# A fused transformer stack on one core: the last sub-layer moved into a third interleaved chain

## The reference

```python
x = x + L0_xattn(ln(x), ctx, ctx, ...)   # 16 heads, each sees every 16th context token
x = x + L0_attn(ln(x), ...)              # causal, scores from distances of 3-d positions
x = x + L0_ffn(ln(x), ...)               # shared expert + 2 of 8 experts per token
x = x + L1_xattn(ln(x), ctx, ...)        # causal + cross attention + feed-forward, 3 norms
x = x + L1_attn(ln(x), ...)              # differential attention, feed-forward
x = x + L1_ffn(ln(x), ...)               # product keys: top 16 of 64 + 64, then of sums
```

```python
sim = jnp.einsum('pbnhd,hkpd->pbnhk', q, keys)       # 2 x 8 heads x 64 keys per token
sx, ix = top_k(sim[0], 16); sy, iy = top_k(sim[1], 16)
scores, pk = top_k(sx[..., :, None] + sy[..., None, :], 16)
h = gelu(x . W_down[pk]) * softmax(scores)
out = sum over heads and picks of h * W_up[pk]
```

## Time and profile before

| | us |
|---|---|
| median of 3 runs | 3579.26 (3578.63 to 3580.27) |
| profiled execution | 3580.67 |
| its span | 3578.7 |
| PE busy | 2692.9 (75%) |
| DVE busy | 1926.9 (54%) |
| ACT busy | 938.1 (26%) |
| POOL busy | 667.2 (19%) |

### The profile page before, as it was taken

How to read it: one execution, slowest core, us unless ns; L and a number is a source line. 1 busy time by engine, 2 the same in 40 slices (tenths; PEclk the granted TensorE clock), 3 DMA queues, 4 the chain that set the end, 5 groups by cost and what they waited for, 6 DMA issues and landing times. The chain is left out here.

```text
span 3578.7 us, 45769 instructions
## 1 busy us (share of the span) xinstructions
PE 2692.9 (75%) x15616; PEld 1884.7 (53%) x15616; DVE 1926.9 (54%) x7470; ACT 938.1 (26%) x2008; POOL 667.2 (19%) x572
## 2 busy tenths in 40 slices
PE   6795898478984889758986689847898489875543
PEld 3583566345762558535674457624586246752421
DVE  2313464844647437554557456484474644664457
ACT  0122242123421233222421234212332123212210
POOL 0102123012211113021140112211231211402040
PEclk9697999788996999969998799978999699985766
DMA  6174054131622226131451406323152223503100
GB/s 223 49 269 157 24 174 148 60 146 46 195 103 104 83 91 210 45 137 48 144 178 38 146 24 209 112 98 110 61 199 84 105 81 115 206 26 111 24 0 6
DMA packets 211632, 392.52 MB, mean 110 GB/s; under 512 B 83344, under 2 KB 163472, under 8 KB 186160
## 3 DMA queue, kind: packets, MB, share of 16 engines
q1 hardware_dynamic: 205232, 372.49, 30.2%
q0 software_dynamic: 6144, 16.79, 1.4%
HBM read 350.55 MB, written 38.67 MB: 109 GB/s over the span
## 5 line engine op out<-in xcount | busy, mean ns | idle before, releaser
L792 PE MATMUL ps<-xbT,stream 128*128 128x128 f32 x2560 | 343.0, 291 | 10.1 <-DMA stream<-in_experts 5.6
L792 PEld LDWEIGHTS ps<-xbT,stream 128*128 128x128 f32 x2560 | 328.1, 205 | 33.8 <-DMA stream<-in_experts 13.7
L299 POOL TENSOR_TENSOR hTB<-pb,sbuf 128x2048 f32<-128x2048 f32 x32 | 151.9, 4759 | 426.5 <-DVE pb L1650 426.5
L607 PE MATMUL ps<-cmat,aTB 128*128 128x512 f32 x256 | 158.3, 776 | 60.8 <-DVE sbuf L1734 57.1
L599 PE MATMUL ps<-ident,xnB 128*128 128x128 f32 x256 | 57.5, 337 | 169.4 <-DVE xnB L1281 125.3
L470 POOL TENSOR_TENSOR rstdA<-veA,mhalf 128x4 f32<-128x4 f32 x24 | 24.4, 1018 | 859.3 <-DVE veA L1274 859.3
L1009 PE MATMUL ps<-ident,work 128*50 128x128 f32 x32 | 12.4, 388 | 220.3 <-DVE work L1789 220.3
L510 POOL DMA_INDIRECT hTA<-y_slots,slot x64 | 62.8, 981 | 601.8 <-DMA y_slots<-yb 584.8
L805 PE MATMUL ps<-stream,hTA 128*128 128x256 f32 x640 | 163.8, 402 | 0.6 <-ACT yb L1139 0.6
L792 PE MATMUL ps<-xbT,ctxA 128*128 128x128 f32 x1280 | 157.8, 277 | 1.4 <-DMA ctxA<-in_experts 1.2
L792 PEld LDWEIGHTS ps<-xbT,ctxA 128*128 128x128 f32 x1280 | 151.4, 192 | 11.4 <-DMA ctxA<-in_experts 5.6
(11 more groups left out here) (277 smaller groups left out, 6132.3 us busy)
## 6 DMA issues: line engine op xcount, KB each, us to landing
stream<-in_experts SPq DMA_DIRECT2D x88, 1024.0 KB, 5.2
stream<-in_experts SPq DMA_DIRECT2D x88, 512.0 KB, 6.0
ctxA<-in_experts SPq DMA_DIRECT2D x40, 1024.0 KB
work<-in_ctxT SPq DMA_DIRECT2D x32, 1028.0 KB, 6.8
hTB<-in_ctxN SPq DMA_DIRECT2D x32, 1024.0 KB, 7.8
down<-in_experts SPq DMA_DIRECT2D x40, 512.0 KB
ctxA<-in_ctxT SPq DMA_DIRECT2D x16, 1024.0 KB, 9.5
stream<-in_ctxT SPq DMA_DIRECT2D x16, 1024.0 KB, 9.1
```

Of the source, the lines that this page charges most:

```text
L299: return e.tensor_tensor(out.rearrange("p (a d h) -> p a d h", a=8, d=16), a.unsqueeze(2).broadcast_to([P, 8, 16, 16]), vals[:, t, :].rear ...
L607: ins = mm(out, aT[:, k, t * P:(t + 1) * P], wt[:, k, cols], start=k == 0, stop=k == KT - 1)
L792: ins = mm(ps[:, 2 * (b % 2) + u, f * P:(f + 1) * P], wu[:, u, k, f * P:(f + 1) * P], xbT[:, b % 2, k, :], start=k == 0, stop=k == KT - 1)
```

## The change

The selection leaves `back()` and becomes a third generator, `peer()`, letter `p`, with 38 steps. `xC` is a new buffer for its residual stream. A pass `g` now runs the front of group g, the back of g-1 and the selection of g-2; at the end of a group with a back VectorE copies `xB` to `xC`. The groups are `f`, `fb` (group 1, outside the loop), six passes of `fbp`, `bp` and `p`: ten in place of nine.

The new `ORDER` begins with three steps of the selection; then each step of the front is followed by two to four of the selection, until the front is in its second norm. There the selection ends and the back starts. So the front's first norm, query and whole cross attention lie between the selection's steps. The second norm and second attention of the front lie between the steps of the back's causal and cross attention; its third norm, router and shared expert lie beside the back's first feed-forward and the norms after it, and its expert blocks beside the back's projections, differential attention and last feed-forward. After the front's last expert block come `f1h6` to `f2h4` of the back, the steps of its last feed-forward, with the front's gather and accumulation between.

`rep64`, `s16`, `cand`, `cm`, `cm2`, `phd` and `u50` now lie in the second half of `hTB`, and `rep1`, `rep2`, `cexp` and `g50` in the second half of `work`. The first halves of `ctxB` and `ctxN` and `ctxL` are loaded at the head of the pass, the second halves once the selection's last `u50` has been turned. Three waits guard the shared buffers where the back follows the selection; some waits of the selection on the back of the same group go away, since a barrier now lies between.

```diff
+        xB, xnB, xC = tiles("xB"), tiles("xnB"), tiles("xC")
...
                 for s in order(streams):
-                    next(front if s == "f" else back)
+                    next({"f": front, "b": back, "p": peer}[s])
...
+                    def first_context():
+                        contextB(0)
                         rows_of(0)
...
+                    def back():
+                        if "p" in streams:
+                            sp.wait_ge(pe_done, PE["uT", T - 1])
+                        else:
+                            first_context()
+                        contextB(1)
+                        rows_of(1)
...
+                    def peer():
+                        if "b" in streams:
+                            first_context()
...
                                 pe.wait_ge(act_done, A["cpT", t])
                                 if t >= 1:
                                     pe.wait_ge(vec_done, V["y1p", t - 1])
+                                elif "p" in streams:
+                                    pe.wait_ge(vec_done, V["x6", T - 1])
...
                             if i == 0:
-                                pe.wait_ge(vec_done, V["h2", "f2", T - 2])
                                 for t in range(T):
...
-                        yield from norm("y0", aTB, (5, 6), None, xB, xnB, smallB)
+                        yield from norm("y0", aTB, (5, 6), ("sim", T - 1) if "p" in streams else None, xB, xnB, smallB)
...
                                 if t >= 2:
                                     act.wait_ge(pe_done, PE["cpv", t - 2])
+                                elif "p" in streams:
+                                    act.wait_ge(pe_done, PE["up", T - 1])
...
-                        yield from norm("n5", xB, xnB, smallB, early=True)
+
+                    def peer():
+                        yield from norm("n5", xC, xnB, smallB, early=True)
...
-                    run(front(), back())
+                    run(front(), back(), peer())
+                    if "b" in streams:
+                        own_steps()
+                        if "p" in streams:
+                            v.wait_ge(out_done, 16 * T)
+                        vv.tensor_copy(xC, xB).then_inc(vec_done, V.step())
...
         group(0, "f")
-        with nc.Fori(1, G) as g:
-            group(g, "fb")
-        group(G, "b")
+        group(1, "fb")
+        with nc.Fori(2, G) as g:
+            group(g, "fbp")
+        group(G, "bp")
+        group(G + 1, "p")
```

## The result

The changed kernel takes 3661.99 us (median of 4 runs, 3653.8 to 3669.27) against 3578.95 beside it on the same chip: a ratio of 1.0239, 95% interval 1.0205 to 1.0272. It is slower by 83 us. The forecast was 3595, its range 3460 to 3690.

What follows compares the result with a forecast made beforehand. Everything was taken to hang on the length of one pass, with VectorE the bound in the selection. 288.2 + 370 + 6 x 419.2 + 334 + 87 = 3594 us of span, forecast 3595 us, 0.4% slower, range 3460 to 3690.

Steps and rivals of the forecast that it cites:

- six passes: Full loop passes of turn, head, neck, body and tail: 419.2 us each, against 422 before.
- fixed price of the new group: Extra group's 87 us, less 52 saved by group 1, and 1 at group 8: 34 us.
- Head: Selection of g-2 with the front's first norm and cross attention; VectorE's work and waits add: 122 us.
- Neck: Back's causal and cross attention with the front's second norm and second attention: 57 us.
- Body: Rest of the back with the rest of the front: 227.4 us of the old middle plus 4.6, 232 us.
- tail: Gathers of expert rows, mostly covered by the back's last feed-forward; last adds and two copies stay: 4 us.
- The term of waits inside a step: VectorE waits in the head's attention steps: value projection 12 us, output projection 4, key projection covered.
- The sign that I had named: In the head, VectorE over 75% busy with waits on the value projection would show the forecast right.
- Small edits: Split context loads, moved writes, added and dropped waits: no effect on the time.
- clock rival: Clock falls at the head, lengthening value and output projections: 15 us a pass, 3685 us; chance 0.2.
- Denser packing: Rival: neck reaches 48.3 us, head and body each hide 6 us of waits: 3456 us; chance 0.35.
- No effect: Rival: a pass of 416.6 us, head and neck 3 us better than summed; chance 0.1.

Runs made afterwards that it cites:

- serial: Changed kernel with all 38 selection steps alone first, then front and back interleaved as in the kernel before: 3650.33 us, ratio 1.0203 to the kernel before.
- split: Changed kernel with the front's six cross-attention steps each cut in three, selection steps between the parts, next scores two steps later: 3575.19 us, ratio 0.9993.
- split_even: split plus two products without a reader after each back cross-attention step, the eighteen parts spread evenly over four row tiles of the selection: 3540.31 us, ratio 0.99.
- even_cold: split_even without the products that have no reader: 3544.81 us, ratio 0.9888 to the kernel before.
- neck_alone: Changed kernel with eighteen back steps (causal and cross attention) alone behind the head, the front's second attention later: 3655.46 us, ratio 1.0216.
- neck_split: split_even with the front's eleven second-attention steps cut in two, each half between back attention steps: 3529.56 us, ratio 0.9858.

## Why the prediction was right or wrong

The direction and the likelier side were right, the size was not: 3652.0 us of span against a sum of 3594. Term by term, measured less forecast: start 285.7 - 288.2 = -2.5; group 1 367.1 - 370 = -2.9; six passes 6 x (429.5 - 419.2) = +61.8; group 8 336.2 - 334 = +2.2; group 9 86.2 - 87 = -0.8. Together +57.8, the whole miss. So the fixed price of the new group and the two end groups were sized well, and everything else is the pass. In it: turn and head +7.0 (133.2 against 126.2), neck +9.7 (66.7 against 57), body -4.3 (227.7 against 232), tail -2.1 (1.9 against 4). That the time is inside the range owes as much to the width of the range, which reached to both rivals, as to the sum.

**Head: right in kind, 7 us short.** The premise that VectorE takes the front's steps in order, so that they add to the selection and do not slip into its gaps, held: serial, with no overlap in the selection at all, is no slower. The term of waits inside a step was right in mechanism and its first item nearly in size: 13.9 us for the value projection (12 forecast), 5.7 for the output projection (4), and 1.8 for the keys, which I had taken as covered. These make 5.4 of the 8.0 us by which this head (130.0) exceeds 122. Another 1.5 are VectorE's own work (95.9 busy, against 69.3 and 25.1 of the chains alone); 1.1 stay unassigned. The sign that I had named, VectorE over 75% busy in the head, was just missed for the same reason: 95.9 of 130.0 is 74%. I had written that nothing can fill these waits. Nothing in this order can; but a cut step can, and split and split_even took them away at 75 us and more in all. That sentence hid the best lever that these runs found.

**Neck: the step that failed.** From ends of 48.3 (perfect cover) and 82.3 (none) I took 57, just over the 54.6 us of TensorE's summed work, which leaves TensorE 2.4 us of idle time. It came to 66.7. The work was less than the sum, 46.6 us on average at a clock of 0.68, but the idle time was 20.1. That is the term that was mis-sized, and it hardly moves: TensorE idles 20.0 to 20.2 us in each of the six necks, at 0.65 as at 0.74, and 20.5 to 20.8 in those of even_cold at up to 0.81. The back alone has 48.3 - 32.6 = 15.7 us of it, 16.3 in neck_alone. The second attention did not fill these gaps; it added 14.0 us of its own work and 3.8 of idle time. An estimate that the earlier trace rows allowed, said after the fact, is the work of both plus the idle time of the longer chain: 54.6 + 15.7 = 70 us. Cutting the second attention's steps left the idle time as it was (17.6 us in split_even and in neck_split), so it does not look like waits inside these steps. What it consists of was not taken apart.

**Body and tail: better than forecast.** The body is as long as the middle of the earlier trace rows, although it took over the expert work; the 4.6 us that I added for it were not needed. The tail of gathers was covered as worked out: the last down projection ends at 1060.95, and the accumulation is over 3.4 us before the copies.

```profile
1059.06 1.89 PE L820 MATMUL ps<-stream,hTA 128*128 128x256 f32 x8
...
1075.11 3.38 DVE L1554 SCALAR_TENSOR_TENSOR xA<-hTA,wpick,xA 128x256 f32<-128x256 f32 x8
1081.91 0.69 DVE L1820 COPY xC<-xB 128x1024 f32<-128x1024 f32 x1
```

**Small edits.** They cost about nothing, as forecast. The wait for `xA` grew from 2.95 to 6.0 us, but it is covered, as shown above. One row shows a cost, TensorE's wait for the second half of `ctxN` in the neck.

```profile
PE ps L903 <- DMA hTB<-in_ctxN: 1.3, 1, 1.3
```

**The rivals.** The time lies nearer to the clock rival (3685) than to the forecast, but its mechanism does not carry it. The granted clock of the head is 0.75, as in the thin stages of before, not near the 0.6 that I named for it, and the two waits that it was to lengthen by 16 us grew by 3.6. (The 74 us of TensorE work that this rival was reckoned from were too few: the head has 86.8.) Where the clock does count is the neck. The same 252 instructions there are busy 48.03 us at 0.65 and 39.75 at 0.81, and that neck is 7.6 us shorter (68.10 against 60.50): all of it is TensorE's own time. But a low clock does not explain why the neck was 9.7 us longer than forecast, since the forecast's 54.6 us are work at 0.61 and 0.63. The clock of the necks was 0.68 on average in the changed kernel, 0.70 in split and 0.80 in even_cold; what raised it there was not isolated. The Trainium skill, page "TensorE: Matmul & The Clock Gate", section "HAM oscillation — how this bites in real kernels", describes such bursts between waits as running slow; the trace agrees for head and neck, at 0.65 to 0.75 rather than the lower level throughout. Denser packing did not happen by itself (neck 66.7, not 48.3); in neck_split the head is below where that rival had it (117.3 with its turn, against 120), and the time is 1.4% under before, not 3.4%, since the neck stays at 62 to 64. No effect is ruled out by the interval.

## What to carry to other kernels

When chains share in-order queues, count a stage as its bounding engine's own work plus every wait inside a step of the partner: such a step is not filler until it is cut where it waits, and here eighteen parts of six steps, laid evenly between the other chain's steps, turned a loss of 2.4% into a gain of 1.1% (even_cold), of which a part came through a higher clock in the next stage. Do not size a stage of two thin chains by TensorE's summed work alone: the idle time that the longer chain has by itself was still there when the second ran beside it. Run each alone and one of them beside dense work, and take the cost that it has there. Before building a third chain, price the extra group that it adds (34 us forecast here, 32 measured) and ask what is left without a dense partner afterwards.

## What the runs showed of the hardware

Products without a reader raised the granted clock and did not pay: in the kernel before, the stage of both cross attentions went from 0.88 to 1.00 and was 74.0 us long in place of 73.5, and the kernel became 0.9% slower. In the changed kernel's necks they raised the clock from 0.68 to 0.81 and left the length as it was. They paid clearly only in group 8, where the back has no partner: 10.6 us less (327.5 against 338.1 us to its last sum), with the clock at 0.70 and 0.71 in place of 0.62 and 0.68.

The spread of a kernel's own runs was larger than I expected and depends on the kernel: split ran from 3554.64 to 3597.9 us in ten runs, neck_split from 3528.19 to 3533.4 in four. In one execution of split the necks of single passes were 63 us at a clock of 0.77 or 69 to 70 at 0.62 to 0.65, with the same instructions; a single profile can be off by such steps, and differences of a few us between two traces are to be read with that in mind.

In the neck a higher granted clock shortened TensorE's busy time and not its idle time: with the same 252 instructions, at 0.65, 0.74 and 0.81, it was busy 48.0, 43.9 and 39.8 us, and idle 20.1, 20.2 and 20.8.
